# Routing of a two-expert LoRA mixture: router logits by one wide matmul, gates brought to expert rows by VectorE's 32x32 block transposes

## The reference, cut to what matters

```python
def cond(x, W, b, A, B, scale, ids):            # adapters, chosen per sequence
    low = einsum('bsi,bri->bsr', x, A[ids])
    return einsum('bsi,oi->bso', x, W) + b + scale[ids] * einsum('bsr,bor->bso', low, B[ids])

def ffn(x, W, b, W_router, lora_A, lora_B):     # 8 experts of rank 16, top 2
    logits = x @ W_router.T                     # tokens x 8
    probs  = softmax(logits)
    p, i   = top_k(probs, 2)                    # a tie goes to the lower index
    p      = p / sum(p)
    w      = sum(one_hot(i, 8) * p[..., None])  # the gate of each expert
    h      = einsum('td,erd->ter', x, lora_A)
    return x @ W.T + b + 2 * einsum('ter,eor,te->to', h, lora_B, w)

x = x + ffn0(cond0(x));  x = x + ffn1(cond1(x))
```

## Time and profile before

| what | value |
|---|---|
| time of the profiled kernel, median of 3 runs | 687.29 us (687.27 to 687.53) |
| span of the profiled execution, first to last instruction | 685.8 us, so 1.5 us lie around it |
| TensorE matmul busy | 680.0 us, 3309 matmuls |
| VectorE busy | 421.5 us, 705 instructions |
| ScalarE busy | 233.5 us, 429 instructions |
| GpSimd busy | 261.3 us, 217 instructions |
| TensorE's granted clock | 1.000 on average |

### The profile page before, as it was taken

One profiled execution on the slowest core, in us unless ns is written; L12 is line 12 of the kernel. 1 busy time (PEld: TensorE's weight loads), 2 busy tenths in 40 slices (PEclk: granted clock), 3 DMA queues, 4 the chain that ended last, 5 costly groups with the idle time before them and its releaser, 6 DMA issues.

```text
span 685.8 us, 9221 instructions
## 1 busy us (share of the span) xinstructions
PE 680.0 (99%) x3309; PEld 600.7 (88%) x3309; DVE 421.5 (61%) x705; ACT 233.5 (34%) x429; POOL 261.3 (38%) x217
## 2 busy tenths in 40 slices
PE   8999999999999999999999999999999999999997
PEld 7999999888888888888899999998888888888886
DVE  5664668768855473862663753886698437738423
ACT  6444245644131034220514344266252302422200
POOL 2373023027593150395133432030647625105920
PEclk9999999999999999999999999999999999999999
DMA  8355756992868934547742755689836886535633
GB/s 298 109 159 180 261 198 209 390 380 108 263 186 321 343 117 130 157 141 258 281 170 72 231 169 183 246 275 375 332 122 216 291 333 195 175 117 171 192 113 122
DMA packets 74131, 147.24 MB, mean 215 GB/s; under 512 B 6948, under 2 KB 38308, under 8 KB 73958
## 3 DMA queue, kind: packets, MB, share of 16 engines
q1 hardware_dynamic: 70678, 138.20, 59.0%
q10 hardware_dynamic: 1872, 6.36, 3.0%
q0 software_dynamic: 1536, 2.10, 1.1%
HBM read 98.42 MB, written 47.33 MB: 213 GB/s over the span
## 4 chain that ended last, share of the span: by engine, by line
PE 97%; DMA 1%; SPq 1%; ACT 0%; DVE 0%; issue 0%
PE ps L599 45%; PE ps L481 15%; PE ps L482 15%; PE ps L483 15%; PE ps L558 4%; PE ps L615 2%; DMA e_raw<-in_ext 1%; PE ps L608 1%; SPq L281 0%; PE ps L498 0%; PE ps L581 0%; ACT e_hl L710 0%; SPq L258 0%; DVE w_hl L972 0%; DVE w L1177 0%; ACT w_hl L719 0%
## 5 line engine op out<-in xcount | busy, mean ns | idle before, releaser
L599 PE MATMUL ps<-x_hl,a_hl 128*128 128x512 f32 x1344 | 317.7, 394 | 0.0
L599 PEld LDWEIGHTS ps<-x_hl,a_hl 128*128 128x128 f32 x1344 | 251.1, 188 | 53.6 <-issue 0.3
L481 PE MATMUL ps<-e_hl,w_hl 128*128 128x384 f32 (+1 forms) x432 | 145.8, 338 | 0.6 <-DVE e_hl L972 0.5
L482 PE MATMUL ps<-e_hl,w_hl 128*128 128x384 f32 (+1 forms) x432 | 145.8, 338 | 0.0
L483 PE MATMUL ps<-e_hl,w_hl 128*128 128x384 f32 (+1 forms) x432 | 145.6, 337 | 0.0
L481 PEld LDWEIGHTS ps<-e_hl,w_hl 128*128 128x128 f32 x432 | 81.5, 189 | 1.8 <-issue 1.0
L482 PEld LDWEIGHTS ps<-e_hl,w_hl 128*128 128x128 f32 x432 | 81.4, 188 | 0.0
L483 PEld LDWEIGHTS ps<-e_hl,w_hl 128*128 128x128 f32 x432 | 81.4, 188 | 0.0
L972 DVE TENSOR_TENSOR x_hl<-x_raw,x_hl 128x512 fp32r<-128x512 f32 x64 | 60.8, 1004 | 8.9 <-ACT x_hl L806 8.9
L1353 POOL TENSOR_TENSOR w<-x_raw 128x512 f32<-128x512 f32 x16 | 23.8, 1515 | 104.6 <-DMA x_raw<-in_xT 34.0
L972 DVE TENSOR_TENSOR w_hl<-w_raw,w_hl 128x1024 fp32r<-128x1024 f32 (+2 forms) x24 | 20.6, 869 | 57.2 <-ACT w_hl L697 50.3
(11 more groups left out here) (115 smaller groups left out, 900.1 us busy)
## 6 DMA issues: line engine op xcount, KB each, us to landing
a_hl<-form_scratch SPq DMA_DIRECT2D x112, 512.0 KB, 5.2
form_scratch<-f_hl SPq DMA_DIRECT2D x56, 512.0 KB, 7.4
e_raw<-in_ext SPq DMA_DIRECT2D x12, 580.0 KB, 8.6
w_raw<-in_w ACTq DMA_DIRECT2D x12, 512.0 KB, 3.3
x_raw<-in_xT SPq DMA_DIRECT2D x6, 1024.0 KB, 8.0
x_raw<-x_scratch SPq DMA_DIRECT2D x6, 1024.0 KB, 7.0
x_scratch<-x_raw SPq DMA_DIRECT2D x16, 256.0 KB, 3.1
out_T<-x_raw SPq DMA_DIRECT2D x16, 256.0 KB, 3.3
```

Of the source, the lines that this page charges most:

```text
L481: nc.tensor.matmul(dst, w_hi, m_hi, start=start, stop=False, skip_group_check=again)
L482: nc.tensor.matmul(dst, w_hi, m_lo, start=False, stop=False, skip_group_check=again)
L599: last = nc.tensor.matmul(ps[:, bank, :], a_hl[:, n % NM, k, w, :], x_hl[:, slot, k, x, :], start=start and i == 0, stop=i == 3 * KH - 1, ...
```

## The change

Logits are now one matmul per chunk in `inner_low`: the stationary operand is the router's 8 columns repeated 16 times over 128 columns (`rt_cols`, made by a ScalarE copy `router_cols`), the moving one the same 512 tokens as for h. Each row of the result in `S_BANK` is thus the logit of expert (row mod 8). VectorE reads the bank with a transpose of 32x32 blocks (512 columns): tokens come to the partitions, 16 groups of 32 columns, of which 8 are used and 8 serve as a second buffer. The ranking is done with reductions and compares over 16 groups of 8, and each quarter of the partitions keeps only its own two experts. The gates are repeated to 16 x 2 x 16 columns, and a second block transpose brings them to expert rows in `hg`. `gated` reads h from PSUM directly. The four small logit matmuls, the four TensorE transposes and the copy `inner` are gone. The lists of VectorE and ScalarE for the second chunk are in a new order, and TensorE runs `low_and_experts(0,1)` for m = 0 and 1 together, behind W3 m = 1.

```diff
@@ inner_low
+                pe.wait_ge(S["rt_done"], u + 1)
+                nc.tensor.matmul(ps[:, S_BANK, :], rt_cols[:], low_mv[tb][:], start=True,
+                                 stop=True).then_inc(S["pe_logit"], 1)
                 nc.tensor.matmul(ps[:, H_BANK, :], stack[tb][:, D:D + ER], low_mv[tb][:], start=False,
@@ product
-                if gates_of is not None:
-                    pe.wait_ge(S["h_done"], 2 * g + gates_of + 1)
-                    pe.wait_ge(S["gate_done"], 2 * g + gates_of + 1)
...
-                    if logits_of is not None and i < TT:
-                        logit = nc.tensor.matmul(ps[:, S_BANK, i * NE:(i + 1) * NE], low_mv[tb][:, i * P:(i + 1) * P],
-                                                 stack[tb][:, D + ER:EXT], start=True, stop=True)
-                    if gates_of is not None and i < TT:
-                        gate = nc.tensor.transpose(ps[:, H_BANK, i * P:(i + 1) * P], gates[:, i, :], ident_sb[:])
@@ tensor, W5 / W3
                         for m in (m2, m2 + 1):
                             pe.wait_ge(S["w5_done"], KH * g + m + 1)
                             product(g, W3, m, BANK_C12[m], False)
-                            if m == 0:
-                                pe.wait_ge(S["hg_lo"], 2 * g + 2)
-                            low_and_experts(0, 1, m, BANK_C12[m])
+                            if m >= 2:
+                                low_and_experts(0, 1, m, BANK_C12[m])
+                        if m2 == 0:
+                            pe.wait_ge(S["hg_lo"], 2 * g + 2)
+                            for m in range(2):
+                                low_and_experts(0, 1, m, BANK_C12[m])
@@ scalar
+            def router_cols(l, g, tb):
...
+                if u:
+                    act.wait_ge(S["hg_done"], u)
+                nc.scalar.copy(rt_cols[:].rearrange("p (n e) -> p n e", e=NE),
+                               stack[tb][:, D + ER:EXT].bitcast(f32).unsqueeze(1).broadcast_to([P, P // NE, NE])
+                               ).then_inc(S["rt_done"], 1)
...
-                    t1_split(g, range(2))
-                    inner(g, 1)
-                    t1_split(g, range(2, 3))
+                    router_cols(l, g, 1)
+                    t1_split(g)
                     top_exp(g, 1)
-                    t1_split(g, range(3, 4))
                     keep_w5(g, 0)
                     hg_split(g, 1)
@@ routing (chain: the next instruction waits for this one, unless False is given)
+                ins = nc.vector.transpose(by_token[:].rearrange("p g c -> p (g c)"), ps[:, S_BANK, :])
+                ins.then_inc(S["logit_read"], 1)
+                dve.wait_ge(S["logit_read"], u + 1)
+                chain(nc.vector.tensor_tensor(lg, lg,
+                                              bias_r[:].unsqueeze(1).broadcast_to([P, GR, NE]), ALU.add))
+                for i, (v, m, gate) in enumerate(((lg, ma, ga), (lg2, mb, gb))):
+                    chain(nc.vector.tensor_reduce(top[i][:], v, AXIS.X, ALU.max))
+                    chain(nc.vector.tensor_tensor(m[:], v, over(top[i], NE), ALU.is_equal))
+                    if i:
+                        sub(gap[:], top[1][:], top[0][:]).then_inc(S["gap_done"], 1)
+                    chain(nc.vector.tensor_tensor(m[:], m[:], ranks, ALU.mult))
+                    chain(nc.vector.tensor_reduce(first_of[i][:], m[:], AXIS.X, ALU.max))
+                    if i == 0:
+                        chain(nc.vector.tensor_tensor(m[:], over(first_of[i], NE), ranks, ALU.is_equal))
+                        chain(nc.vector.scalar_tensor_tensor(lg2, m[:], -3.0e38, lg, op0=ALU.mult, op1=ALU.add), False)
+                    chain(nc.vector.tensor_tensor(gate[:], over(first_of[i], WANT), wanted, ALU.is_equal))
                 dve.wait_ge(S["exp_done"], u + 1)
                 chain(nc.vector.tensor_scalar(den[:], ex[:], 1.0, None, ALU.add))
                 chain(nc.vector.reciprocal(wb[:], den[:]))
                 chain(nc.vector.tensor_scalar(wa[:], wb[:], 2.0, None, ALU.mult))
+                chain(nc.vector.tensor_tensor(den[:], ex[:], wa[:], ALU.mult), False)
+                chain(nc.vector.tensor_tensor(ga[:], ga[:], over(wa, WANT), ALU.mult))
+                chain(nc.vector.tensor_tensor(gb[:], gb[:], over(den, WANT), ALU.mult))
+                chain(nc.vector.tensor_tensor(by_token[:].rearrange("p g (n r) -> p g n r", r=R),
+                                              *(m[:].unsqueeze(3).broadcast_to([P, GR, WANT, R]) for m in (ga, gb)),
+                                              ALU.add))
+                chain(nc.vector.transpose(hg[:], by_token[:].rearrange("p g c -> p (g c)")))
@@ vector, list of a pair
                     low_rest(g, 1)
+                    made_split(g, T1)
                     out_c11(g, 2)
                     out_c11(g, 3)
-                    made_split(g, T1, range(2))
+                    sum_split(g, T3, w57)
                     routing(g, 1)
-                    made_split(g, T1, range(2, 4))
-                    sum_split(g, T3, w57)
-                    for m in range(KH):
+                    gated(g, 1)
+                    keep_u2(g, 0)
+                    gated_low(g, 1)
+                    for m in range(1, KH):
                         keep_u2(g, m)
-                    gated(g, 1)
```

More of the change, by code:

```diff
@@ L39 @@
 SUPER = NCH // 2
+SQ = 32
+GR = CH // SQ
+WANT = SQ // R
 CHAIN = 13
@@ L185, in fused_layers @@
         assert 2 * E_PITCH <= 5 * CH
-        gates = place("gates", [P, TT, ER], f32, at[0] - CH * 4)
-        h_sb = place("h_sb", [P, CH], f32)
+        by_token = place("by_token", [P, GR, SQ], f32)
+        rt_cols = place("rt_cols", [P, P], f32r, at[0] - CH * 4)
         low_b = place("low_b", [LOW, CH], f32)
@@ L193, in fused_layers @@
         ident_sb = place("ident_sb", [P, P], f32)
-        iota_sb = place("iota_sb", [P, TT, NE], f32)
+        ones_sb = place("ones_sb", [P, P], f32r)
+        ma = place("ma", [P, GR, NE], f32)
+        mb = place("mb", [P, GR, NE], f32)
+        ga = place("ga", [P, GR, WANT], f32)
+        gb = place("gb", [P, GR, WANT], f32)
+        iota_sb = place("iota_sb", [P, NE], f32)
+        rank_sb = place("rank_sb", [P, NE], f32)
+        want_sb = place("want_sb", [P, WANT], f32)
         smask_sb = place("smask_sb", [2 * LOW, BPC], f32)
-        ones_sb = place("ones_sb", [P, P], f32r)
         scale_sb = place("scale_sb", [2 * LOW, BATCH], f32)
@@ L205, in fused_layers @@
         ids_sb = place("ids_sb", [1, LAYERS * BATCH], mybir.dt.int32)
[L206 to L216, removed]
+        lg, lg2 = (by_token[:, :, i * NE:(i + 1) * NE] for i in range(2))
+        top = [place(f"top{i}", [P, GR, 1], f32) for i in range(2)]
+        first_of = [place(f"first_of{i}", [P, GR, 1], f32) for i in range(2)]
+        gap = place("gap", [P, GR, 1], f32)
+        ex = place("ex", [P, GR, 1], f32)
+        den = place("den", [P, GR, 1], f32)
+        wa, wb = first_of
         assert at[0] <= nc.sbuf_usable_end, at[0] - nc.sbuf_usable_end
@@ L806, in x_split, with t1_split @@
                     nc.scalar.copy(x_hl[:, slot, k, 0, :], raw_of(block, k)).then_inc(x_hi[block], 1)
-            def t1_split(g, ks):
+            def t1_split(g):
                 slot = SLOT_OF[g % SUPER][T1]
-                for k in ks:
+                for k in range(KH):
                     act.wait_ge(S["t1_done"], KH * g + k + 1)
@@ L856, in first_stack @@
                     ins.then_inc(S[done], 1)
[L858 to L862, removed]
+                    if done == "stack_in":
+                        router_cols(l, SUPER * l, 0)
             def top_exp(g, tb):
@@ L930, in _ @@
                     if s:
+                        router_cols(l, g, 0)
                         x_split(l, g, B12)
@@ L1137, in routing, with over @@
                 u = 2 * g + tb
+                ranks = rank_sb[:].unsqueeze(1).broadcast_to([P, GR, NE])
+                wanted = want_sb[:].unsqueeze(1).broadcast_to([P, GR, WANT])
+                def over(v, n):
+                    return v[:].broadcast_to([P, GR, n])
                 dve.wait_ge(S["pe_logit"], u + 1)
-                chain(nc.vector.tensor_tensor(lg[:], ps[:, S_BANK, 0:TT * NE].rearrange("p (t e) -> p t e", t=TT),
-                                              bias_r[:].unsqueeze(1).broadcast_to([P, TT, NE]), ALU.add))
@@ L1141, in routing @@
[L1141 to L1151, removed]
@@ L1244, in _ @@
                         if l == 0:
+                            chain(nc.vector.tensor_scalar(rank_sb[:], iota_sb[:], -1.0, float(NE), ALU.mult, ALU.add))
+                            for q in range(P // SQ):
+                                chain(nc.vector.tensor_copy(want_sb[q * SQ:(q + 1) * SQ, :],
+                                                            rank_sb[q * SQ:(q + 1) * SQ, q * WANT:(q + 1) * WANT]))
                             sub(sign_sb[STACK:P, :], halves_sb[STACK:P, 0:1], halves_sb[STACK:P, 1:2])
```

(1 more changed line is left out.)

53 lines of the change are left out of this document (23 added, 30 removed).

## The result

The changed kernel takes 706.54 us (median of 4 runs, 704.24 to 708.0) against 687.28: a ratio of 1.0275, 95% interval 1.0263 to 1.0287. It is slower, as forecast, but by 19.3 us where 9.8 were forecast, and lies outside the range.

The account below looks back on a forecast made before the run. TensorE was taken as the bound, busy 680.0 of 685.8 us. Four pairs x (3.86 of stalls - 1.42 of matmuls saved) = +9.8 us on 687.3 gave 697 us, range 690 to 704.

Parts of the forecast that it names:

- TensorE's own sum, -5.7: TensorE, all four pairs: small logit matmuls and transposes removed save 7.5 us, new logit matmuls add 1.8.
- The routing, 7.4 us: VectorE's new routing: a mostly chained list of instructions, summed to 7.3 and taken as 7.4 us, bounds 5.9 to 8.8.
- Place and mechanism of the two waits: Second chunk of each pair: W3 1 waits for keep_w5 1, W3 2 for keep_w5 2 queued behind T4's last copy.
- Their size, 3.9 us for both stalls of a pair: TensorE's waits at W3 1 and W3 2 together: 648.85 - 644.99 = 3.9 us per pair, the first 1.1.
- the 1.30 that I carried over: Second chunk, VectorE: low part of hg, sharing SBUF with GpSimd, taken at 1.30 us as in the kernel before.
- a rival at 0.08: TensorE's clock falls in the new stalls, 3.0 us lost in each of four pairs, time 709; chance 0.08.
- My price of 3.0 per fall: Clock rival: loss per fall, from the start, where nine matmuls take 4.21 us, 0.45 each, against 0.227 later.
- Behind it nothing more is late: After the W3 2 wait: out_c12 for W7 2, add_21, add_22, SP's ring loads and W4's T4 all come in time.
- First chunk: Pair 0's longer routing is done by 150.5, TensorE needs it at 153.7: hidden by 3.2 us, no wait.

Follow-up runs that it names:

- The SP order: SP's ring loads 22 to 25 ahead of the out_c12 stores and next B21 load; alone against the changed kernel 705.51 us, against the kernel before 687.58.
- both ScalarE moves: Changed kernel with ScalarE's second-chunk list reordered: keep_w5 0, 1; hg_split; keep_w5 2, 3; t4_split; 693.75 us.
- three moves: Changed kernel with keep_w5 1 before hg_split, keep_w5 2 and 3 before t4_split, and SP's ring loads 22 to 25 ahead of the out_c12 stores; 683.14 us.

## Why the prediction was wrong

- **TensorE's own sum, -5.7: right within 1 us.** With the waits gone the span is 681.0, 4.8 below the one before, and TensorE's busy time falls by 5.4.
- **The routing, 7.4 us: right.** 7.44 in pairs 0 and 3. A block transpose of 512 columns takes 0.71 from PSUM and from SBUF, an instruction of 128 values 0.29. The Trainium skill, Vector Engine (DVE) Microarchitecture Reference, section 3.8, has the block transpose at one element per cycle per lane; the trace agrees, with 0.71 against 0.69 to 0.75 for the other instructions over 512 columns.
- **Place and mechanism of the two waits: right.** In pair 3 each step is within 0.7 us of its forecast when counted from W6: routing ends at 18.8 (18.7), last T4 copy starts at 32.5 (32.1), W3 2 starts at 33.6 (33.3).
- **Their size, 3.9 us for both stalls of a pair: too small,** 4.0 in pairs 1 and 3, 4.6 in pairs 0 and 2. I read one pair, the last, where 3.9 was near. In pairs 0 and 2 the T1 and `low_rest` subtractions meet GpSimd more (T1 takes 5.8 us there against 5.3). The low part of `hg` takes 1.82 in every pair, not the 1.30 that I carried over. Over four pairs 1.8 us, and about 1 for slow first matmuls that I had not priced.
- **The failed step: the sum has no term for the clock. It stands only as a rival at 0.08, set aside because "the waits of about 1 and 3 us have matmuls on both sides".** It is not an alternative to the waits but a surcharge on them. It came in three of four pairs of the profiled run, in addition to all the waits: 4.8 us there, 3.5 to 7.1 over the runs (span times one minus clock). With it the excess over the forecast is accounted for: of 8.7 us in the profiled run (18.5 against 9.8) the clock makes 4.8, the waits' size 1.8, slow first matmuls 1, the ring load 0.5 and the time outside the span 0.5. Without the clock's share the profiled run would have taken 701 us, inside the range of 690 to 704. My price of 3.0 per fall was for a whole passage at the start of the program, where the profile gives the granted clock as 1.00 and only the pace of 0.45 us per matmul spoke for a lower one; here a tile lost 1.6 to 2.6. The Trainium skill, TensorE: Matmul & The Clock Gate, section on oscillation, says that recurring waits can throw the array back each time; the trace agrees in part, behind three of the four second waits and none of the four first ones. I had set it aside for want of a row.
- **"Behind it nothing more is late": right for the changed kernel** but for one ring wait of 0.2 us. It did not hold once the stalls were taken out by ScalarE's list: then the ring loads behind the store of `out_c12` were late, in part because T4's copies now stood behind `keep_w5` 3 (2.5 us). The SP order is worth nothing in the kernel before, nothing clear in the changed one, and 10.6 us with both ScalarE moves.
- **First chunk: right,** no wait there.

What stays open: why the clock stayed up in pair 0 after 2.73 us and fell in pair 2 after 2.71 in one and the same run, while with SP's order alone the same wait of pair 0 halved it for a whole tile. So how often it falls in a run I could not have forecast. Open is also what makes the half microsecond more outside the span.

## What to carry to other kernels

When TensorE is the bound, price a new wait as the wait and the clock behind it, and look at each repetition of the stage, not at one. Follow a late result through every list that it stands in: here the cure was not a faster routing but three moves, so that copies and loads that did not need the late data no longer stood behind it, and the last of them alone was worth nothing clear. A move in a list also makes the moved work wait for what now stands ahead of it, as T4's copies did for `keep_w5` 3. Removing small matmuls is then worth their distance of starts (7.5 us by the earlier trace rows, of which 1.8 go to the new ones), and not their busy time (14.1).

## What was not expected of the hardware

Short waits of TensorE between matmuls were at times enough for the granted clock to fall behind them. In the traces of the changed kernel and of its variants, one execution each, counting TensorE's waits in front of a product's matmul:

| wait of TensorE | how often the clock fell behind it |
|---|---|
| 1.0 to 1.9 us | 0 of 24 |
| 2.1 to 2.3 us | 3 of 5 |
| 2.5 to 2.8 us | 6 of 12 |
| 3.8 to 4.1 us | 6 of 6 |

In the changed kernel a fall cost the tile behind it 1.6 us (0.61 to 0.63 over 4.4 us); with SP's order alone it cost 2.6 us in pair 0 (0.50 over 5.3 us), after a wait of 2.73 us. So the cost did not go by the length of the wait alone. A VectorE subtraction of 512 columns that starts together with GpSimd's `add_12` took 1.82 us, three times its time alone.
